# Expert jobs of 256 instead of 512 token slots in the last phase of a two-layer network

## The reference

```python
gates = softmax(xt @ gate_w)                      # 4096 tokens, 8 experts
top_v, top_i = top_k(gates, 2)
top_v = top_v / top_v.sum(-1)
h  = gelu(einsum('nd,edf->enf', xt, fc_w))        # 256 -> 1024, for each expert
eo = einsum('enf,efd->end', h, proj_w)            # 1024 -> 256
out = sum over the token's two experts of eo * top_v
```

## Time and profile before

| | us |
|---|---|
| median of three runs | 5777.41 |
| the profiled execution | 5808.26 |
| its span, first to last instruction | 5806.4 |
| mean granted TensorE clock, share of full speed | 0.862 |
| expert phase, up to the first job | 4867 to 5023 |
| the jobs | 5023 to 5684 |
| gather and last normalisation | 5684 to 5806 |

### The profile page before, as it was taken

One profiled execution on the slowest core, in us unless ns is written; L12 is line 12 of the kernel. 1 busy time (PEld: TensorE's weight loads), 2 busy tenths in 40 slices (PEclk: granted clock), 3 DMA queues, 4 the chain that ended last, 5 costly groups with the idle time before them and its releaser, 6 DMA issues. The chain is left out here.

```text
span 5806.4 us, 82633 instructions
## 1 busy us (share of the span) xinstructions
PE 4852.6 (84%) x20772; PEld 1699.4 (29%) x20772; DVE 3830.3 (66%) x4276; ACT 3417.0 (59%) x3983; POOL 3980.6 (69%) x2256
## 2 busy tenths in 40 slices
PE   5449998998999889889979998998899785399991
PEld 3211112222222222222222222222222344266661
DVE  7848888777887788788878887887888403000003
ACT  4536666777677767777777767777767512111111
POOL 2359998998899789889979897998889200400004
PEclk7755558998999899899989998998999895699995
DMA  2357766776667566666756775666677221333322
GB/s 89 94 172 254 240 233 222 253 255 221 242 236 265 202 234 245 230 223 235 260 214 232 247 254 199 251 242 241 228 235 261 81 76 41 113 117 109 108 101 94
DMA packets 313082, 1139.77 MB, mean 196 GB/s; under 512 B 69664, under 2 KB 123424, under 8 KB 306720
## 3 DMA queue, kind: packets, MB, share of 16 engines
q1 hardware_dynamic: 298688, 1065.24, 52.5%
q0 software_dynamic: 13920, 69.22, 3.6%
HBM read 1077.17 MB, written 69.73 MB: 198 GB/s over the span
## 5 line engine op out<-in xcount | busy, mean ns | idle before, releaser
L1542 POOL TENSOR_TENSOR s_h<-s_decay,s_h 128x768 f32<-128x768 f32 x2048 | 3703.9, 1842 | 444.9 <-ACT s_decay L1197 407.1
L1580 DVE TENSOR_TENSOR s_h<-s_h,bank 128x1024 f32<-128x1024 f32 x2048 | 2473.0, 1216 | 531.6 <-PE bank L803 305.0
L1197 ACT ACTIVATE s_decay<-s_decay,s_a_neg 128x1536 f32<-128x1536 f32 x1024 | 1605.5, 1568 | 246.9 <-DMA s_decay<-dt_rows 245.7
L829 PE MATMUL bank<-s_h,s_cdiag 128*32 128x512 f32 x8192 | 1275.6, 699 | 4.2 <-ACT s_y L1209 4.2
L1202 ACT ACTIVATE bank<-bank,s_a_neg 128x512 f32<-128x512 f32 x1024 | 672.4, 657 | 743.5 <-PE bank L817 740.7
L803 PE MATMUL bank<-s_vrow,s_brow 9*128 9x512 bf16 x4096 | 845.1, 425 | 208.9 <-DVE s_h L1580 167.2
L1570 DVE TENSOR_TENSOR s_h<-bank,s_h 128x512 f32<-128x512 f32 x1024 | 699.2, 683 | 2.8 <-ACT bank L1202 2.7
L927 PE MATMUL bank<-m_ma,m_w 128*128 128x512 f32 x1024 | 579.4, 659 | 44.7 <-ACT m_mb L1273 39.3
L803 PEld LDWEIGHTS bank<-s_vrow,s_brow 9*128 9x128 bf16 x4096 | 203.3, 92 | 1407.0 <-issue 1403.7
L941 PE MATMUL bank<-m_mb,m_w 128*128 128x512 f32 x1024 | 581.0, 660 | 30.9 <-ACT m_ma L1278 17.5
L817 PE MATMUL bank<-s_drow,s_unit 3*128 3x512 bf16 x1024 | 436.9, 427 | 74.2 <-DMA s_drow<-dt_parts 49.2
(11 more groups left out here) (195 smaller groups left out, 4201.1 us busy)
## 6 DMA issues: line engine op xcount, KB each, us to landing
s_decay<-dt_rows SPq DMA_DIRECT2D x1024, 768.0 KB, 5.1
m_w<-in_units SPq DMA_DIRECT2D x210, 512.0 KB, 5.3
s_vrow<-v_parts SPq DMA_DIRECT2D x1024, 36.0 KB
s_brow<-b_parts SPq DMA_DIRECT2D x1024, 9.0 KB
v_parts<-p_part SPq DMA_DIRECT2D x24, 512.0 KB, 3.0
slots<-in_x_tiles SPq DMA_DIRECT2D x128, 96.0 KB, 5.2
e_xs<-slots SPq DMA_DIRECT2D x24, 512.0 KB
expert_out<-e_made SPq DMA_DIRECT2D x23, 512.0 KB, 9.2
```

Of the source, the lines that this page charges most:

```text
L829: mm = pe.matmul(bank[q * 32:(q + 1) * 32, Y0], cdiag[:, hf * LANES + q, at * BLK:(at + 1) * BLK], h[:, t % 2, hf * LANES + q], start=(at ...
L1197: act.activation(decay[:, k % RING], decay[:, k % RING], ACT.Exp, scale=a_neg[:, 1:2]).then_inc(decay_ok, 1)
L1542: pool.tensor_tensor(h[:, t % 2, g * PAIR:(g + 1) * PAIR, DCOLS:], decay[:, k % RING, g % 2 * PAIR:(g % 2 + 1) * PAIR], h[:, (t + 1) % 2, ...
L1580: dve.tensor_tensor(h[:, t % 2, g * PAIR:(g + 1) * PAIR], h[:, t % 2, g * PAIR:(g + 1) * PAIR], bank[:, X0 + n % 2 * PAIR:X0 + (n % 2 + 1) ...
```

## The change

A job has `JOB` = 256 slots, that is `JT` = 2 tiles of 128. `JOBS` becomes 32 + 8 = 40 and `RUN` 39, so the slots worked on go from 23 x 512 = 11776 to 39 x 256 = 9984. An expert can now have up to `MOST` = 16 jobs, and so many comparisons count them. `turn` has 4 transposes, `up` 8 products of 2 matmuls with 256 moving columns, two of them side by side in one bank with one GELU of 512 columns behind them, and `down` 2 products of 8 matmuls, both in bank 4 + j % 2, with one copy. Each job still fetches 1 MB of `fc` and 1 MB of `pj`. `xs` has four buffers and is loaded four jobs ahead. The job loops of PE, ACT, DVE and SP are written out for all 39 jobs. PE's order becomes `turn(j)`, `down(j-1)`, `up(j)`, so that `down(j-1)` comes right behind `up(j-1)` and `turn(j)`. Counts of semaphores follow; `SLOTS_FILL` writes 80 rows at a time.

```diff
-JOBS = 2 * BATCH + EXPERTS
+JOB = 256
+JT = JOB // P
+JOBS = 2 * BATCH * SEQ // JOB + EXPERTS
+MOST = BATCH * SEQ // JOB
...
+XS = 4
...
-        xs = sb("e_xs", [P, 2, TT, DIM])
+        xs = sb("e_xs", [P, XS, JT, DIM])
         cT = sb("e_cT", [P, 2, KD, SEQ])
-        hid = sb("e_hid", [P, 2, KH, SEQ])
-        made = sb("e_made", [P, 2, TT, DIM])
+        hid = sb("e_hid", [P, 2, KH, JOB])
+        made = sb("e_made", [P, 2, JT, DIM])
...
-            for j in range(2):
+            for j in range(XS):
...
-                sp.wait_ge(made_ok, LEAD + 2 * (j + 1))
+                sp.wait_ge(made_ok, LEAD + j + 1)
                 hold(sp, sp_passed)
                 sp.wait_ge(made_out, 16 * (j + 1))
                 sp.sem_inc(made_free, 1)
                 sp.dma_start(d["EXPERT_OUT_TILES"][j], made[:, slot_]).then_inc(made_out, 16)
 
-            with sp.Fori(0, (RUN - 1) // 2) as it:
-                for r in range(2):
-                    j = it * 2 + r
+            for j in range(RUN):
+                if j + XS < RUN:
                     sp.wait_ge(T_ps, LEAD + j + 1)
                     hold(sp, sp_passed)
-                    sp.dma_start(xs[:, r], d["SLOT_TILES"][j + 2]).then_inc(xs_in[r], 16)
-                    store(j, r)
-            store(RUN - 1, (RUN - 1) % 2)
+                    sp.dma_start(xs[:, j % XS], d["SLOT_TILES"][j + XS]).then_inc(xs_in[j % XS], 16)
+                store(j, j % 2)
...
-                    pool.wait_ge(up_ps, LEAD + (j - 1) * KH)
+                    pool.wait_ge(up_ps, LEAD + (j - 1) * (KH // 2))
...
-                    pool.wait_ge(down_ps, LEAD + (j - 1) * 2)
+                    pool.wait_ge(down_ps, LEAD + j - 1)
...
-            def turn(j, r, n):
-
-                pe.wait_ge(xs_in[r], 16 * (n + 1))
+            def turn(j):
+
+                pe.wait_ge(xs_in[j % XS], 16 * (j // XS + 1))
                 pe.wait_ge(T_a, LEAD + j)
                 pe.wait_ge(T_v, LEAD + j)
                 for k in range(KD):
-                    for i in range(TT):
-                        mm = pe.transpose(bank[:, T0 + k, i * P:(i + 1) * P], xs[:, r, i, k * P:(k + 1) * P],
+                    for i in range(JT):
+                        mm = pe.transpose(bank[:, T0 + k, i * P:(i + 1) * P], xs[:, j % XS, i, k * P:(k + 1) * P],
                                           w["ident"][:])
                 mm.then_inc(T_ps, 1)
...
-                    pe.wait_ge(up_ok, LEAD + j * KH + m + 1 - 4)
-                    product(bank[:, m % 4], lambda k: fc[:, r, k * HID + m * P:k * HID + (m + 1) * P],
-                            lambda k: cT[:, 0, k], KD).then_inc(up_ps, 1)
+                    if m % 2 == 0:
+                        pe.wait_ge(up_ok, LEAD + j * (KH // 2) + m // 2 + 1 - 4)
+                    mm = product(bank[:, m // 2, m % 2 * JOB:(m % 2 + 1) * JOB],
+                                 lambda k: fc[:, r, k * HID + m * P:k * HID + (m + 1) * P],
+                                 lambda k: cT[:, 0, k, 0:JOB], KD)
+                    if m % 2 == 1:
+                        mm.then_inc(up_ps, 1)
 
             def down(j, r, n):
 
                 pe.wait_ge(pj_in[r], 16 * (n + 1))
-                pe.wait_ge(up_ok, LEAD + (j + 1) * KH)
-                for half in range(2):
-                    pe.wait_ge(made_ok, LEAD + 2 * j + half + 1 - 2)
-                    for i in (2 * half, 2 * half + 1):
-                        mm = product(bank[:, D0 + half, i % 2 * DIM:(i % 2 + 1) * DIM],
-                                     lambda k: hid[:, r, k, i * P:(i + 1) * P],
-                                     lambda k: pj[:, r, k * DIM:(k + 1) * DIM], KH)
-                    mm.then_inc(down_ps, 1)
-
-            turn(0, 0, 0)
+                pe.wait_ge(up_ok, LEAD + (j + 1) * (KH // 2))
+                pe.wait_ge(made_ok, LEAD + j + 1 - 2)
+                for i in range(JT):
+                    mm = product(bank[:, D0 + r, i * DIM:(i + 1) * DIM],
+                                 lambda k: hid[:, r, k, i * P:(i + 1) * P],
+                                 lambda k: pj[:, r, k * DIM:(k + 1) * DIM], KH)
+                mm.then_inc(down_ps, 1)
+
+            turn(0)
             up(0, 0, 0)
-            turn(1, 1, 0)
-            with pe.Fori(0, (RUN - 1) // 2) as it:
-                j = it * 2 + 1
-                up(j, 1, it)
-                turn(j + 1, 0, it + 1)
-                down(j - 1, 0, it)
-                up(j + 1, 0, it + 1)
-                turn(j + 2, 1, it + 1)
-                down(j, 1, it)
+            for j in range(1, RUN):
+                turn(j)
+                down(j - 1, (j - 1) % 2, (j - 1) // 2)
+                up(j, j % 2, j // 2)
             down(RUN - 1, (RUN - 1) % 2, (RUN - 1) // 2)
...
-                act.activation(cT[:, 0, 0], bank[:, T0], ACT.Copy).then_inc(T_a, 1)
+                act.activation(cT[:, 0, 0, 0:JOB], bank[:, T0, 0:JOB], ACT.Copy).then_inc(T_a, 1)
 
             def gelu(j, r):
-                act.wait_ge(down_ps, LEAD + 2 * (j - 1))
-                for m in range(KH):
-                    act.wait_ge(up_ps, LEAD + j * KH + m + 1)
-                    act.activation(hid[:, r, m], bank[:, m % 4], ACT.Gelu).then_inc(up_ok, 1)
+                act.wait_ge(down_ps, LEAD + j - 1)
+                for m in range(KH // 2):
+                    act.wait_ge(up_ps, LEAD + j * (KH // 2) + m + 1)
+                    act.activation(hid[:, r, 2 * m:2 * m + 2].rearrange("p m t -> p (m t)"), bank[:, m], ACT.Gelu
+                                   ).then_inc(up_ok, 1)
 
             turned(0)
             gelu(0, 0)
-            turned(1)
-            with act.Fori(0, (RUN - 1) // 2) as it:
-                for r in range(2):
-                    gelu(it * 2 + 1 + r, (r + 1) % 2)
-                    turned(it * 2 + 2 + r)
+            for j in range(1, RUN):
+                turned(j)
+                gelu(j, j % 2)
...
-            for m in range(1, BATCH):
+            for m in range(1, MOST):
...
-                dve.tensor_copy(cT[:, 0, 1], bank[:, T0 + 1]).then_inc(T_v, 1)
+                dve.tensor_copy(cT[:, 0, 1, 0:JOB], bank[:, T0 + 1, 0:JOB]).then_inc(T_v, 1)
...
             def result(j, r):
                 dve.wait_ge(made_free, LEAD + j)
-                for half in range(2):
-                    dve.wait_ge(down_ps, LEAD + 2 * j + half + 1)
-                    dve.tensor_copy(made[:, r, 2 * half:2 * half + 2].rearrange("p i d -> p (i d)"),
-                                    bank[:, D0 + half]).then_inc(made_ok, 1)
+                dve.wait_ge(down_ps, LEAD + j + 1)
+                dve.tensor_copy(made[:, r].rearrange("p i d -> p (i d)"), bank[:, D0 + r]).then_inc(made_ok, 1)
 
             dve.wait_ge(made_out, 16)
             turned(0)
-            turned(1)
-            with dve.Fori(0, (RUN - 1) // 2) as it:
-                for r in range(2):
-                    turned(it * 2 + 2 + r)
-                    result(it * 2 + r, r)
+            for j in range(1, RUN):
+                turned(j)
+                result(j - 1, (j - 1) % 2)
             result(RUN - 1, (RUN - 1) % 2)
...
-        slots = nc.dram_tensor("slots", (JOBS * SEQ, DIM), F32, kind="Internal").ap()
-        outs = nc.dram_tensor("expert_out", (RUN * SEQ, DIM), F32, kind="Internal").ap()
+        slots = nc.dram_tensor("slots", (JOBS * JOB, DIM), F32, kind="Internal").ap()
+        outs = nc.dram_tensor("expert_out", (RUN * JOB, DIM), F32, kind="Internal").ap()
```

More of the change, by code:

```diff
@@ L1866, in expert_phase @@
         scattered, all_out, eps_ok = sem("e_scattered"), sem("e_all_out"), sem("e_eps_ok")
-        xs_in = [sem(f"e_xs_in{k}") for k in range(2)]
+        xs_in = [sem(f"e_xs_in{k}") for k in range(XS)]
         fc_in = [sem(f"e_fc_in{k}") for k in range(2)]
@@ L2122, in _ @@
             dve.tensor_scalar(jobs[:, 0], total, 0.0, None, ALU.is_gt).then_inc(jobs_ok, 1)
-            for m in range(1, BATCH):
+            for m in range(1, MOST):
                 dve.wait_ge(jobs_ok, m)
-                dve.scalar_tensor_tensor(out=jobs[:, 0], in0=total, scalar=float(m * SEQ), in1=jobs[:, 0],
+                dve.scalar_tensor_tensor(out=jobs[:, 0], in0=total, scalar=float(m * JOB), in1=jobs[:, 0],
                                          op0=ALU.is_gt, op1=ALU.add).then_inc(jobs_ok, 1)
-            dve.wait_ge(jobs_ok, BATCH)
+            dve.wait_ge(jobs_ok, MOST)
             dve.tensor_tensor_scan(jobs[:, 1], w["ones"][:, 0:EXPERTS], jobs[:, 0], 0.0, ALU.mult, ALU.add
                                    ).then_inc(jobs_ok, 1)
-            dve.wait_ge(jobs_ok, BATCH + 1)
+            dve.wait_ge(jobs_ok, MOST + 1)
             dve.tensor_tensor(jobs[:, 2], jobs[:, 1], jobs[:, 0], ALU.subtract).then_inc(jobs_ok, 1)
@@ L2141, in _ @@
             dve.tensor_scalar(rows[:], whose[:], w["pcol"][:, 0:1], None, ALU.add).then_inc(rows_ok, 1)
-            dve.wait_ge(jobs_ok, BATCH + 2)
+            dve.wait_ge(jobs_ok, MOST + 2)
```

(8 more changed lines are left out.)

## The result

The kernel after takes 5702.7 us (median of four runs, 5696.57 to 5721.52), the one before 5775.5 in the same comparison: a ratio of 0.9873, with an interval of 0.9852 to 0.9894. That is 72.8 us less, where 73.7 were forecast. The profiled execution took 5696.6 us with a span of 5694.8.

The account below looks back on a forecast made before the run. PE was taken to bound the jobs. Slots -98.6, pauses +25.8, start -1.2, ahead and behind +1.7 and -1.4 sum to -73.7 us, off the median of 5777.4: 5703.7 us, range 5682 to 5728.

Parts of the forecast that it names:

- Step 1, fewer slots: PE in the jobs: up and down records at 216 ns, 39 jobs in 556.0 us instead of 654.6, minus 98.6 us.
- the upper bound of 406 ns: Price of an up record on PE if its weight load were not hidden at all, 216 + 190 ns.
- Step 2, the pause: PE before every down waits for the last GELU: 0.65 us for 38 jobs, with the last job plus 25.8 us.
- Steps 3 to 6, start, ACT and DVE, weights, SP: Start of the jobs: one pause of 0.8 us replaces two, minus 1.2 us; the other engines and fetches cost nothing.
- step 6: SP's queue of stores and `xs` loads, written out: loads are for four jobs later, so it costs nothing.
- Step 7, ahead and behind: Outside the jobs: more comparisons and rows plus 1.7 us, shorter first load and last store minus 1.4 us.
- No pause: Rival, 5%: transposes and PE's queue hide the GELU's chain before down, 24.7 us go, 5679 us.
- The clock: Rival, 4%: PE's 38 short stops each let the clock fall, costing 122 us, 5826 us.
- The weights: Rival, 3%: a job's two fetches go one after the other, 18.0 us a job, 5821 us.
- The written-out program: Rival, 3%: fetching PE's unrolled instructions, 22 packets at 5.0 us of wait each, costs 110 us, 5814 us.

Follow-up runs that it names:

- e3: Kernel after with PE's old order, up(j), turn(j+1), down(j-1), at 256 slots; the jobs took 560.7 us, ratio to before 0.9839.
- e10: Kernel after with jobs of 128 slots, 71 of them; the jobs took 572.3 us, ratio to before 0.9853.
- e9: Kernel after, but down does 6 of its first tile's 8 matmuls before waiting for the last GELU; jobs 559.8 us, ratio to before 0.9845.
- e6: Kernel after with two token buffers in place of four; the jobs took 581.1 us, ratio to before 0.985.
- the second: Comparison in which the kernel after was run again without any edit against the kernel before; ratio 0.9875, jobs 581.1 us.
- e1: Kernel before run again without any edit, for a second trace; its one run took 5785 us, with a tail of 100.5 us.
- e8: Kernel after with two more 1 MB weight fetches a job into spare buffers nothing reads; jobs 581.0 us, ratio to before 0.9876.
- e11: Kernel after with 128-slot jobs, and down doing 4 of 8 matmuls before waiting for the last GELU; 5629.7 us, ratio to before 0.9742.
- e5: Kernel after with its job loops not written out and two token buffers; the jobs took 583.3 us, ratio to before 0.9869.

## Why the prediction was right

*Step 1, fewer slots.* Right in price, wrong in one reason. Up records came 216 ns apart, and a job without its pause takes 14.25 us (e3), 14.26 forecast. But I excluded the upper bound of 406 ns by "190 ns hide under 216", and e10 shows that the load's duration sets no such limit: records can be 112 ns apart under loads of 192. That the down record had the same shape was the sound half of the argument.

*Step 2, the pause.* The mechanism was right and was the one that two experiments removed (e3, e9); the size was off. Forecast 0.65 us a job, measured 0.53, so 4.6 us over 38 jobs. The term at fault is the release of PE: I took 0.26 us from DVE's copy, and the GELU's release by ACT took 0.10, so the wait is 0.46 us instead of 0.62. The longer down behind it took back 0.04 of that (0.07, where I had 0.03). DVE's release is still 0.24 in the chain after (its copy at 5015.32 with 0.44, up at 5016.00). The jobs came to 581.0 us instead of 585.8 (556.0 + 25.8 + 3.2 + 0.8).

*Steps 3 to 6, start, ACT and DVE, weights, SP.* No wait, as forecast. The first up took 9.35 us, 2.4 more than a steady one, against the 2.1 taken over from before, and the first turn 0.7 more (1.10 instead of 0.44) against 1.1, as it is half as long: 3.1 together, where 3.2 was taken. The first pause was 0.77. The four token buffers of step 6 were not needed (e6). No other wait of PE appears in the jobs:

```profile
PE bank L2002 <- issue: 99.0, 1, 99.0
PE bank L1961 <- issue: 12.0, 39, 0.7
PE bank L1961 <- DVE e_cT L2167: 0.8, 1, 0.8
```

*Step 7, ahead and behind.* The comparisons took 2.97 us for 15 instead of 1.37 for 7, the 1.6 forecast; the last store's DMA 2.13 instead of 2.93 us, 0.8 where 0.7 was estimated. From the issue of the first `xs` load to the first transpose it was 2.7 and 2.9 us in the two traces of after, 4.0 and 3.9 in those of before, so 1.0 to 1.3 where 0.7 was estimated.

*The sum.* -73.7 forecast, -79 by the jobs, -72.8 by the medians of the first comparison and -77 by those of the second (5704.2 against 5781.3). The nearness of the forecast to the median is partly luck: the jobs came out 4.8 us lower, and the median of the kernel before moves by up to 5.8 us from one comparison to the next (5775.5 to 5781.3). The interval of the ratio, 61 to 85 us, holds both -73.7 and -79, so the medians can't tell them apart and only the traces can. Taking the difference off the median and not off the one profiled execution was what mattered: that execution had 22 us of chance in its tail (e1).

*The rivals.* No pause: false, 0.53 us, though e3 and e9 show what that case looks like: some 20 us less. The clock: granted 1.00 in 400 us with 28 pauses of 0.30 us, and 1.00 with the 50 of 0.52 us in the same window of e10. By the rule of the Trainium skill on short idling ("TensorE: Matmul & The Clock Gate", section A second HAM failure mode: psum-queue depth-cycling) the clock would have swung; the traces do not show it for pauses of this size. The weights: PE did not wait for them at 178 GB/s, nor at 320 with two fetches more (e8), nor at 327 in e11. The written-out program: q8 brought 21 packets in the jobs, where 22 were estimated, and none made PE wait; the loops of e5 are no faster.

## What to carry to other kernels

Where work is padded to a fixed job size, count what the padding costs on the bounding engine: here it was the whole gain, and with the late wait the gain went on at half the size again (559.8 to 518.5 us for the jobs), where the operands fetched for each job kept the DMA engines 94% busy. When a job shrinks, look for the chain that does not shrink with it (here a GELU over a full bank with its two hand-overs, 0.90 us) and for what covers it; asking for the last piece only where it is used cost nothing here and gave back all of it. Price a matmul by the distance between the starts of records of the same shape, never by its duration or that of its weight load.

## What was not expected of the hardware

- Weight loads of 190 ns each under matmuls 112 ns apart (e10).
- The hand-over to PE took 0.10 us from ACT and 0.24 to 0.26 from DVE, in the same program. Whether that is the engine or the instruction is open.
- 327 GB/s over 400 us, of which four fifths of the DMA engines' time (82%) went to gathers of 8 KB rows, with no wait of PE for the weights (e11).
- Two waits of some 22 us each in the tail of one execution of before that no other trace shows; their cause stays open.
